# Expert results: scattered to token rows by GpSimd in the expert steps, instead of stored in sorted order and gathered in the heads

## The reference, cut to what matters

```python
# x: (1, 2048, 256)
xn = layernorm(x)
# attention: 16 heads of 16 dims, rope on q and k; each query attends to the first 205
# and the last 512 key positions (717 of 2048)
attn = softmax(where(allowed, q @ k.T / 4, -big)) @ v      # per head
out1 = concat(attn) @ Wo.T + bo
# experts: 8 experts, 256 -> 176 -> 256; each token uses the expert with the best logit only
logits = xn @ router_w.T
top2 = top_k(logits, 2);  weight = softmax(top2)[:, 0];  expert = top2_index[:, 0]
y[e] = (silu(xn @ gate_w[e].T) * (xn @ up_w[e].T)) @ down_w[e].T
return x + out1 + weight * y[expert]
```

## Time and profile before

| | |
|---|---|
| time, median of 3 runs | 395.14 us (394.01 to 395.59) |
| the profiled execution's own time | 396.47 us |
| its span, first to last instruction of the program | 394.7 us |
| time around the span | 1.8 us |
| expert steps, first to last result copy on ACT | 53.7 to 116.0 us |
| heads, from the first scores of head 0 | from 116.43 us |
| output projection and stores | from 377.3 us |
| granted TensorE clock, mean over the span | 0.996 |

### The profile page before, as it was taken

How to read it: one execution, slowest core, us unless ns; L and a number is a source line. 1 busy time by engine, 2 the same in 40 slices (tenths; PEclk the granted TensorE clock), 3 DMA queues, 4 the chain that set the end, 5 groups by cost and what they waited for, 6 DMA issues and landing times.

```text
span 394.7 us, 12245 instructions
## 1 busy us (share of the span) xinstructions
PE 370.9 (94%) x4646; PEld 194.1 (49%) x4646; DVE 322.2 (82%) x549; ACT 270.2 (68%) x537; POOL 65.6 (17%) x82
## 2 busy tenths in 40 slices
PE   0999999999999999999999999999999999997896
PEld 0765566766655443444444444445454444432265
DVE  5769789997759888988888888888888898874566
ACT  2534666564448878778787787878888888886910
POOL 5003734431000213032130321300000000000000
PEclk9999999999999999999999999999999999998999
DMA  7998556755111213032130321302102022095626
GB/s 238 407 384 215 145 169 200 215 171 157 41 58 54 70 32 95 11 94 63 41 88 14 99 55 46 92 11 71 55 21 70 25 52 56 17 204 105 101 54 213
DMA packets 30920, 42.53 MB, mean 108 GB/s; under 512 B 10724, under 2 KB 25700, under 8 KB 30048
## 3 DMA queue, kind: packets, MB, share of 16 engines
q1 hardware_dynamic: 29000, 36.71, 32.5%
q0 software_dynamic: 1872, 5.11, 5.1%
HBM read 27.75 MB, written 13.67 MB: 105 GB/s over the span
## 4 chain that ended last, share of the span: by engine, by line
PE 83%; DMA 5%; DVE 4%; issue 3%; ACT 2%; SPq 2%; DVEq 0%; ACTq 0%
PE ps L735 19%; PE ps L713 18%; PE ps L653 17%; PE ps L601 7%; PE ps L528 5%; PE ps L614 5%; PE ps L772 4%; DVE mx L1025 3%; DMA softmax_sums<-o_st 2%; DMA bqk<-bqk_in 2%; PE ps L639 2%; PE ps L517 1%; PE ps L587 1%; PE ps L626 1%; PE ps L510 1%
## 5 line engine op out<-in xcount | busy, mean ns | idle before, releaser
L1025 DVE TENSOR_REDUCE mx<-ps 128x1 f32<-128x717 f32 x232 | 198.6, 899 | 30.6 <-PE ps L653 30.1
L735 PE MATMUL ps<-q_op,k_op 98*32 98x512 bf16 (+1 forms) x1472 | 129.7, 383 | 3.6 <-DMA q_op<-neg_row 1.6
L1307 ACT ACTIVATE probs<-ps 128x512 f32<-128x512 f32 x192 | 103.1, 598 | 19.9 <-PE ps L735 18.1
L653 PE MATMUL ps<-k_op,q_op 96*32 96x512 bf16 (+1 forms) x1856 | 111.2, 315 | 0.4 <-DVE mx L1025 0.3
L653 PEld LDWEIGHTS ps<-k_op,q_op 96*32 96x32 bf16 x1856 | 50.7, 96 | 56.3 <-issue 25.3
L735 PEld LDWEIGHTS ps<-q_op,k_op 98*32 98x32 bf16 (+1 forms) x1472 | 42.3, 96 | 67.0 <-ACT probs L1307 15.0
L713 PE MATMUL ps<-probs,v_op 128*32 128x512 f32 x384 | 50.6, 595 | 0.2 <-ACT o_st L1298 0.2
L1307 ACT ACTIVATE dn<-ps 77x512 f32<-77x512 f32 x64 | 34.8, 595 | 11.6 <-PE ps L735 11.6
L457 POOL COPY v_op<-v_all 128x192 f32<-128x192 f32 x16 | 7.0, 446 | 202.7 <-PE ps L713 202.7
L1307 ACT ACTIVATE gu<-ps 128x512 f32<-128x512 f32 x64 | 34.5, 599 | 9.1 <-PE ps L735 9.1
L1307 ACT ACTIVATE wqk<-ps 128x512 f32<-128x512 f32 x64 | 33.5, 599 | 8.1 <-PE ps L735 8.1
(11 more groups left out here) (127 smaller groups left out, 366.0 us busy)
## 6 DMA issues: line engine op xcount, KB each, us to landing
q_parts<-parts SPq DMA_DIRECT2D x12, 256.0 KB
sorted_results<-ys SPq DMA_DIRECT2D x23, 128.0 KB
q_op<-q_parts SPq DMA_DIRECT2D x15, 192.0 KB
gu<-gu_in SPq DMA_DIRECT2D x1, 2816.0 KB, 13.7
tab<-tab_in SPq DMA_DIRECT2D x1, 2048.0 KB, 11.6
sorted_rows<-xn SPq DMA_DIRECT2D x4, 512.0 KB, 6.1
out<-x_sb SPq DMA_DIRECT2D x8, 256.0 KB, 2.4
q_op<-q_parts SPq DMA_DIRECT2D x15, 128.0 KB
```

Source lines behind the costliest of these rows:

```text
L653: ins = pe.matmul(ps[r:r + CW, at + c0:at + c0 + n], q_op[slot][0:KR, P * t + r:P * t + r + CW], k_op[slot][0:KR, c0:c0 + n], start=True, ...
L735: ins = pe.matmul(bank(4 + u % RING)[r:r + w, :], k_op[k][:, c0 + r:c0 + r + w], q_op[k][:, QB * b:QB * b + QB], start=True, stop=True)
L1025: dve.tensor_reduce(mx[:, slot, t:t + 1], ps[:, at:at + NK], AX.X, ALU.max).then_inc(max_reduced, 1)
L1307: act.activation(prob[c][0:rows, QB * b:QB * b + QB], bank(4 + u % RING)[0:rows, :], ACT.Exp, scale=SCALE).then_inc(exp_done, 1)
```

## The change: what it does

Each result tile is no longer stored in sorted order but scattered: POOL issues an indirect DMA per slot whose destination row in `y_dram` is `result_row`, the token's number plus one. For this the token numbers are counted from 1 (`iota` with base 1), so that padded lanes have the sum 0 and write row 0, which no one reads. `token_of` is the same sum less one, and at least zero. Rows 1 to 2048 of `y_dram` are then the results in token order. SP loads them plainly, in four pieces of 4 x 128 rows: two after the work of head 0 and two after that of head 1.

POOL's order in the expert steps becomes: gathers 0 to 7, then in turn gather t and scatter t-8, then the last eight scatters. Scatter t waits for its result (`ys_ready`) and for the landing of scatter t-1. The biases are added in the same heads as before, without the gathers. SP waits for the landing of all scatters once, before it loads the first results. DVE's end phase waits for the four loads instead of the sixteen gathers.

```diff
@@ constants and buffers
+LAG = 8
-        token_of = sb("token_of", [P, NSLOT], U32)
+        token_of, result_row = (sb(n, [P, NSLOT], U32) for n in ("token_of", "result_row"))
@@ sync
-            def store_ys(t):
-                sp.wait_ge(ys_ready, t + 1)
-                sp.dma_start(y_dram[t * P:t * P + P, :], ys[t % XR][:]).then_inc(ys_stored[t % XR], 16)
+            def load_results(g):
+                rows = y_dram[1 + 4 * P * g:1 + 4 * P * (g + 1), :].rearrange("(t p) d -> p t d", p=P)
+                sp.dma_start(y_tok[:, 4 * g:4 * g + 4, :], rows).then_inc(results_in, 16)
             for s in range(2, NSLOT):
-                store_ys(s - 2)
                 for u, part in STORE_AT.get(s, ()):
...
             load_neg(0, 0)
-            for t in range(NSLOT - 2, NSLOT):
-                store_ys(t)
             head_step(0, 0, first=True)
+            for n in range(XR):
+                sp.wait_ge(ys_stored[n], 16 * len(range(n, NSLOT, XR)))
+            for g in range(2):
+                load_results(g)
             head_step(1, 1)
+            for g in range(2, 4):
+                load_results(g)
@@ gpsimd
-            pool.iota(token_id[:], [[P, NT]], base=0, channel_multiplier=1).then_inc(iota_ready, 1)
+            pool.iota(token_id[:], [[P, NT]], base=1, channel_multiplier=1).then_inc(iota_ready, 1)
-            for t in range(NSLOT):
+            def scatter(t):
+
+                pool.wait_ge(ys_ready, t + 1)
+                if t > 0:
+                    pool.wait_ge(ys_stored[(t - 1) % XR], ((t - 1) // XR + 1) * 16)
+                pool.indirect_dma_start(
+                    out=y_dram, out_offset=bass.IndirectOffsetOnAxis(ap=result_row[:, t:t + 1], axis=0),
+                    in_=ys[t % XR][:], in_offset=None
+                ).then_inc(ys_stored[t % XR], 16)
+
+            for t in range(LAG):
                 gather(t)
-                if t == 6:
+                if t == LAG - 2:
                     pool.wait_ge(v_read, NCH)
...
-            pool.wait_ge(route_ready, 1)
-            pool.wait_ge(lo_ready, NPROJ)
-            for n in range(XR):
-                pool.wait_ge(ys_stored[n], 16 * len(range(n, NSLOT, XR)))
+            pool.wait_ge(result_row_ready, 1)
+            for t in range(LAG, NSLOT + LAG):
+                if t < NSLOT:
+                    gather(t)
+                scatter(t - LAG)
+
-            def gather_result(t):
-
-                pool.indirect_dma_start(
-                    out=y_tok[:, t, :], out_offset=None, in_=y_dram,
-                    in_offset=bass.IndirectOffsetOnAxis(ap=row_of[:, t:t + 1], axis=0)
-                ).then_inc(gathered, 16)
+            def add_bias(t):
                 pool.tensor_tensor(x_sb[:, t, :], x_sb[:, t, :], bvo[:, HID:2 * HID], ALU.add
                                    ).then_inc(residual_ready, 1)
@@ vector
-                dve.tensor_copy(token_of[:], slot_sums).then_inc(token_ready, 1)
+                dve.tensor_scalar(token_of[:], slot_sums, -1.0, 0.0, ALU.add, ALU.max).then_inc(token_ready, 1)
+                dve.tensor_copy(result_row[:], slot_sums).then_inc(result_row_ready, 1)
...
-            dve.wait_ge(gathered, 16 * NT)
+            dve.wait_ge(results_in, 16 * 4)
```

More of the change, by code:

```diff
@@ L208, in layer @@
         ones_ready, id16_ready, iota_ready = sem("ones_ready"), sem("id16_ready"), sem("iota_ready")
-        lane_ready, slot_ready, slots_summed, token_ready = (
-            sem(n) for n in ("lane_ready", "slot_ready", "slots_summed", "token_ready"))
+        lane_ready, slot_ready, slots_summed, token_ready, result_row_ready = (
+            sem(n) for n in ("lane_ready", "slot_ready", "slots_summed", "token_ready", "result_row_ready"))
         xn_stored, residual_ready, expert_ready = sem("xn_stored"), sem("residual_ready"), sem("expert_ready")
@@ L218, in layer @@
             sem(n) for n in ("hid_turned", "hidT_ready", "down_done", "ys_ready"))
-        gathered = sem("gathered")
+        results_in = sem("results_in")
         qk_loaded, v_loaded = sem("qk_loaded"), sem("v_loaded")
@@ L487, in _ @@
                 for t in range(2 * (h - RING), min(2 * (h - RING) + 2, NT)):
-                    gather_result(t)
+                    add_bias(t)
         @block.tensor
```

## The result

| | before | after |
|---|---|---|
| time, median | 395.19 us (394.01 to 395.59, 4 runs) | 407.5 us (406.9 to 409.18, 4 runs) |
| ratio after / before | | 1.0335, 95% interval 1.0298 to 1.0371 |
| profiled execution, its span | 396.47, 394.7 us | 409.18, 407.4 us |
| first and last result copy on ACT | 53.7, 116.0 us | 54.5, 127.5 us |
| head 0 starts | 116.43 us | 127.93 us |

A forecast was written before the change was run, and what follows sets the result against it. The prediction took PE, busy 94% of the span, to bound the kernel. It summed -4.7 (heads 3 to 10), +4.0 (chain), +0.6 (scatters in head 0) and +0.3 (result loads) to +0.2 us: 395.3 us, range 390.8 to 401.0.

The forecast's parts named there:

- the chain's delay: Expert steps: the last result copy, and head 0 with it, come 4.0 us late, at 120.0 instead of 116.0.
- Part 1: Heads 3 to 10: removing sixteen POOL gathers ends the delay of PE's signals, worth 4.7 us (bounds 0 to 4.9).
- Part 2: Expert steps: 23 stores become scatters in one chain on POOL, each waiting for the last to land; 4.0 us late.
- the period P: Scatter chain on POOL, issue, transfer, completion and wake: 3.7 us loaded (3.2 to 4.3), 2.8 quiet (2.5 to 3.3).
- with 0.5 for completion: Scatter chain: completion and POOL's wake after the transfer take 0.5 us, giving 2.8 us per quiet period.
- the bound of 1.1: Scatter chain: upper bound of 1.1 us for completion and wake, from a gather that let SP go on 4.3 us later.
- Rival (b): Scatter chain slower, by the padded row or a 1.1 us completion: delay 6.6 to 12.3, total 397.9 to 403.6; chance 0.19.
- The delay of 14 us: Expert steps: head 0's delay with the chain's periods at 4.3 us loaded and 3.3 quiet.
- PE's rows come no later than this: Expert steps: gather t follows scatter t-9, with more room than the copy, so PE's rows are no later than the copies.
- The 0.6 us for these: Head 0: scatters 19 to 22 run inside it at 0.3 us each, 0 to 1.2 us, taken at 0.6.
- Part 3: SP without stores: earlier loads gain nothing; scatters in head 0 cost 0.6 us, result loads 0.3 (bounds 0 and 2).
- Part 4: DVE's token_of in two steps and one more copy cost 0.1 us, hidden in PE's projections; end phase finds data loaded.

The follow-up runs named there:

- e2: Changed kernel with SP's wait for the scatters and the four result loads moved after head 13: 411.69 us, ratio 1.0428 to the kernel before.
- f1: Kernel before without its sixteen gathers, adds left in place, results loaded in sorted order in heads 2, 5, 8 and 11: 390.41 us, ratio 0.9864.
- f2: Kernel before with its sixteen bias adds moved behind POOL's last copy of v, so gathers stand alone in heads 3 to 10: 409.03 us, ratio 1.0333.
- f4: Changed kernel with destination rows t*128 + lane in place of the tokens' rows, so no row is written twice: 407.34 us, ratio 1.0307.
- e1: Changed kernel with 20 result buffers in place of 4, same order on POOL: 406.81 us, ratio 1.0272 to the kernel before.
- e3: Changed kernel with 20 result buffers, gathers 15 slots ahead of scatters instead of 8, result loads after head 13: 400.25 us, ratio 1.0126.
- e4: Changed kernel without the wait for the scatter before, slots scattered into four DRAM tensors in turn: 398.58 us, ratio 1.0099 to the kernel before.
- h2: Changed kernel with a plain store on POOL, no index, in place of each scatter, in the same chain: 392.84 us, ratio 0.9937.
- g1: Changed kernel with 20 result buffers, gathers 15 slots ahead, one result load each in heads 2, 5, 8 and 11: 392.77 us, ratio 0.9918.

## Why the prediction was wrong

**The sum.** Forecast +0.2 us, measured +12.7 in the spans: the chain's delay 11.5 for 4.0, head 0 3.7 for 0.6, the result loads 3.9 for 0.3 (against e2's head 2), the heads' gain right at -4.7, and -1.7 at the end that was not in the sum.

**Part 1 held.** -4.7 was forecast. Heads 1 to 8 take 132.8 us before; after, with head 2 taken at e2's 16.0 us, 112.1 + 16.0 = 128.1: 4.7 less. f1 gives the whole, 5.2 us between the two medians. The reason held too: in head 5 PE's transpose, which was L660 in the earlier trace rows, has no idle time ahead of it although POOL's adds are still in the head.

```profile
223.70 0.22 PE L670 MATMUL ps<-id,neg 128*32 128x128 bf16 x1
```

What I couldn't say, gather or add, f1 and f2 settle for the gather.

**Part 2 failed, in the period P.** The mechanism, its place and its signs were those named: POOL waiting for the scatter before, ACT idle ahead of its copies. The size was off, term by term. The forecast had the last copy at 120.0; it came at 127.5:

- Scatter 0 started at 55.2 and not at 54.2: 1.0, of which 0.8 was there before any scatter (first copy at 54.5 for 53.7; over the kernels shown here it ranges from 52.7 to 55.1 us, so that is no effect of the change).
- Twelve loaded cycles took 102.61 - 55.16 = 47.4 us, 3.95 each and not 3.7: 3.0.
- Six cycles to scatter 18 took 123.85 - 102.61 = 21.2 us and not 18.6: 2.6. P in the quiet was put at 2.8, with 3.3 as the upper bound. It is 3.15, 3.9 behind a slot that is mostly padding, and 3.97 behind slot 15, beside the loads of head 2. The transfer was well estimated (2.3 us; the packets of the scatter of 131.42 were through within 2.1). What failed is "with 0.5 for completion": it is 1.1 us, or 1.8 on padded slots. The 0.5 was taken from nothing that wrote to DRAM; the bound of 1.1 was there.
- Landing and wake at the end, 127.51 - 123.85 = 3.7 for 2.8: 0.9. This is slot 18, not a padded one, and its cycle of 4.33 us is the longest of the quiet ones. Slot 16's landing had released ACT after 2.48 us (116.86 to 119.34), with all packets through 2.0 us after the issue. Of slot 18's the last three came between 126.0 and 127.1 us, up to 3.1 us after it, and a packet of q8 ran in between, from 125.34:

```profile
q8 instruction: 1, 0.02, 4.0%
```

```profile
q0 software_dynamic: 3, 0.01, 4.0%
```

(The first row is of 125.2 to 126.4 us, the second of 126.0 to 127.1.) f4 and e2 have the same at slot 18, with cycles of 4.72 and 4.93 us. So some 1.2 us of the delay of head 0 go with such a packet, which fell into the last scatter that head 0 waited for. That is seen in three traces and was not isolated by a run; no term of the sum had it.


Together 7.5. Rival (b) had the padded row and the slow completion, but as alternatives, and a delay of 6.6 to 12.3 for them; 11.5 lies in it. Its total of up to 403.6 stayed low for want of the next two points. The delay of 14 us that the working gives for the upper ends does not come out of its own terms: 54.2 + 10 x 4.3 + 9 x 3.3 = 126.9, a delay of 10.9, less than was measured. The sentence that gathers have more room than copies and so "PE's rows come no later than this" was wrong: e1, with the copies freed, still took 67.8 us from first to last copy for 62.3, 5.5 more.

The Trainium skill (DMA: Bandwidth & Descriptors, Anatomy of one DMA — SWDGE (gpsimd) path) puts most of the fixed 2 us into the receipt of the write in the target memory, and says HBM is the heaviest. The 1.1 us from the last packet to POOL's next scatter are of that kind, though a third of the cycle and not most of it; the 2.3 us that the page's fit gives for the whole, an estimate, are short of the 3.15 here and of the 2.49 of a plain store.

**Head 0: a second price of a wait.** I counted a delay as a delay. In a stretch where PE was busy 2.3 of 6 us the granted clock fell to 1.2 GHz, and 8 us of head 0 ran at it. Across the kernels this goes with the waits and not with the scatters in head 0: with the clock at 0.77 to 0.79 head 0 takes 18.5 to 19.3 us (after, e2), at 1.00 it takes 15.5 to 16.1 (e1, e3, e4, h2, g1), with one to five scatters or POOL stores beside it. The 0.6 us for these was of the right size at most: nothing in e3 (15.50), 0.2 in g1 (15.67), 0.6 in e1 (16.14).

**Part 3 failed in one half.** The first pair of loads stood before head 1 and was free, as said. Of the second pair I wrote that PE needs the loads of head 4 some 8 us into the head, and took 0.3 for both. SP comes to them only when head 0's reciprocals are done, 163.42 us, which is already the start of head 2; 1.4 us more of issue and 1 MB in front, and PE waited 2.15 us at 173.4 and its clock dipped to 0.91. Head 2 lost 3.9 us by it, so the bound of 2 us was too low as well. Single loads of 512 KB ahead of the reciprocals' wait cost nothing (f1; heads 5 and 8 of g1).

**Part 4 held.** DVE's two instructions of 23 columns take 0.18 and 0.17 us.

**The end.** The cause of the -1.7 us from head 9 on is open: 0.8 of it is head 14 (15.74 us for 16.51) and 1.2 what comes behind it (32.43 for 33.64). Head 14 takes 14.7 to 16.7 us from kernel to kernel, by when the sums of head 13 land.

## What to carry to other kernels

A chain of DMAs in which each waits for the landing of the one before needs its period from a landing that was seen, at both ends: measure issue to next issue, not issue to last packet. If it can't keep up, decouple it before giving it up: more buffers and the other users of its queue ahead of it, with the result loads moved, made 407.5 us into 392.8 here (ratios to the kernel before 1.0335 and 0.9918). In front of PE a wait can cost twice, once as idle time and once at half clock, and where loads may stand in a queue is decided by which wait they come before and after.

## What the runs showed of the hardware

- Indirect DMAs issued by POOL slow the other engines though they share no data with them: gathers 0.3 us each at 2 us apart, 0.7 each in pairs without a pause, 1.3 each in a row of twelve (the fallen clock included), in which PE, ACT and DVE nearly stop; scatters 3 us and more apart between nothing and 0.4 us each.
- A chained store of 128 KB to DRAM takes 1.87 us per link on SP, 2.49 as a plain DMA on POOL, 3.15 as a scatter, and 3.9 when most of the 128 rows are the same one.
- A scatter beside which a packet of the queue "instruction" ran had its last packets 3.1 us after the issue for 2.0, and the chain's cycle was 4.33 us for 3.15 (4.72 and 4.93 in f4 and e2).
- A tensor_scalar of 16 columns on DVE took 6.30 us for 0.17 while POOL ran additions; reductions beside it weren't touched.
